# Third layer of a four-layer attention kernel: the self attention's values projected between its first steps, and queries that wait only for their own normed tokens

## The reference, cut to what matters

```python
def attention(x, ctx, ng, nbv, ncg, ncb, wq, wkv, wo, bo, rel_emb):
    xn = layer_norm(x, ng, nbv)
    cn = layer_norm(ctx, ncg, ncb)
    q = xn @ wq
    kv = cn @ wkv
    k, v = jnp.split(kv, 2, axis=-1)
    ...
    sim = jnp.einsum('bhnd,bhmd->bhnm', q, k)
    sim = (sim + rel_pos_bias(rel_emb, n, m)) * SCALE
    attn = jax.nn.softmax(sim, axis=-1)
    out = jnp.einsum('bhnm,bhmd->bhnd', attn, v)
    ...
    return out @ wo + bo
x = attention(x, x, sa_norm_g, ...) + x
x = attention(x, context, ca_norm_g, ...) + x
```

## Time and profile before

| what | value |
|---|---|
| median of 3 runs | 4007.54 us (3999.14, 4007.54, 4008.92) |
| the profiled execution's own time | 4000.44 us |
| its span, first to last instruction | 3998.7 us |
| TensorE busy | 3681.9 us, 92% of the span |
| VectorE, ScalarE, GpSimd busy | 1997.7 us, 1717.6 us, 381.1 us |
| mean clock granted to TensorE | 0.953 of full speed |
| turns of the third layer | between 2111 and 3230 us of the span, some 149 us each |

### The profile page before, as it was taken

How to read it: one execution, slowest core, us unless ns; L and a number is a source line. 1 busy time by engine, 2 the same in 40 slices (tenths; PEclk the granted TensorE clock), 3 DMA queues, 4 the chain that set the end, 5 groups by cost and what they waited for, 6 DMA issues and landing times. The chain is left out here.

```text
span 3998.7 us, 67495 instructions
## 1 busy us (share of the span) xinstructions
PE 3681.9 (92%) x21816; PEld 2836.5 (71%) x21816; DVE 1997.7 (50%) x6075; ACT 1717.6 (43%) x4729; POOL 381.1 (10%) x471
## 2 busy tenths in 40 slices
PE   7999999999979999999978999999999996888888
PEld 5878787877758888888756666666666664666666
DVE  3644555455525555555543454454454544555454
ACT  3544454444523433333314545545545552333333
POOL 1101110110011111111000000000000001111110
PEclk9999999999979999999989999999999997989898
DMA  5000000000030000000011000000000000000000
GB/s 177 4 11 14 14 4 11 14 12 6 1 114 11 12 12 12 12 12 10 3 42 44 8 7 14 8 7 14 8 7 14 7 1 26 13 12 12 20 15 5
DMA packets 69151, 75.08 MB, mean 19 GB/s; under 512 B 17537, under 2 KB 66561, under 8 KB 67841
## 3 DMA queue, kind: packets, MB, share of 16 engines
q1 hardware_dynamic: 68864, 71.42, 5.9%
HBM read 64.01 MB, written 7.40 MB: 18 GB/s over the span
## 5 line engine op out<-in xcount | busy, mean ns | idle before, releaser
L161 PE MATMUL l_bank<-l_xT,weights_of_layers_and 128*128 128x224 f32 x2816 | 625.5, 376 | 40.5 <-DMA weights_of_layers_and<-in_L_xattn_w_fused 11.8
L161 PEld LDWEIGHTS l_bank<-l_xT,weights_of_layers_and 128*128 128x128 f32 x2816 | 552.6, 202 | 70.5 <-DMA weights_of_layers_and<-in_L_xattn_w_fused 12.1
L614 ACT ACTIVATE l_pT<-l_bank 125x336 f32<-125x336 f32 (+2 forms) x608 | 290.8, 478 | 287.0 <-PE l_bank L546 276.7
L546 PEld LDWEIGHTS l_bank<-identity,l_p 112*125 112x125 f32 (+2 forms) x1952 | 272.8, 174 | 155.6 <-issue 77.8
L546 PE MATMUL l_bank<-identity,l_p 112*125 112x112 f32 (+2 forms) x1952 | 321.7, 277 | 24.6 <-DVE l_p L593 20.0
L161 PE MATMUL l_bank<-l_cT,weights_of_layers_and 128*128 128x375 f32 x832 | 319.9, 515 | 4.7 <-DVE l_z L1815 3.7
L335 PE MATMUL l_bank<-l_cv,l_pT 125*112 125x17 f32 (+1 forms) x2304 | 268.3, 247 | 45.5 <-ACT l_pT L377 44.1
L335 PEld LDWEIGHTS l_bank<-l_cv,l_pT 125*112 125x112 f32 x2304 | 261.1, 180 | 52.6 <-DVE l_O L419 26.6
L313 PEld LDWEIGHTS l_bank<-identity,l_p 112*125 112x125 f32 (+1 forms) x1408 | 218.7, 184 | 111.3 <-ACT l_p L373 11.2
L161 PE MATMUL l_bank<-weights_of_layers_and,l_cT 128*125 128x256 f32 (+2 forms) x960 | 295.7, 448 | 0.1
L728 POOL TENSOR_TENSOR l_ve<-l_mv,eps 112x2 f32<-112x2 f32 (+1 forms) x89 | 17.5, 196 | 2607.6 <-DVE l_mv L722 2607.6
(11 more groups left out here) (255 smaller groups left out, 6264.3 us busy)
## 6 DMA issues: line engine op xcount, KB each, us to landing
l_cx<-in_ctx SPq DMA_DIRECT2D x32, 375.0 KB
l_cT<-in_ctx_turned SPq DMA_DIRECT2D x32, 375.0 KB, 3.5
x_after_layer<-l_z SPq DMA_DIRECT2D x24, 224.0 KB, 2.4
l_x<-x_after_layer SPq DMA_DIRECT2D x24, 224.0 KB, 2.7
weights_of_layers_and<-in_L_xattn_w_fused SPq DMA_DIRECT2D x1, 2048.0 KB, 8.8
weights_of_layers_and<-in_L_xattn_w_ff SPq DMA_DIRECT2D x1, 2048.0 KB, 12.1
weights_of_layers_and<-in_L_xattn_lin_W SPq DMA_DIRECT2D x2, 1024.0 KB, 10.2
weights_of_layers_and<-in_L_xattn_sa_wkv SPq DMA_DIRECT2D x1, 2048.0 KB, 14.7
```

The lines of the kernel that those rows point to most:

```text
L161: last = pe.matmul(out, left, right, start=(k == 0), stop=(k == len(pairs) - 1))
L546: last = pe.transpose(TR.bank(m)[:ph.keys, g * ph.rows:(g + 1) * ph.rows], p[:ph.rows, m % self.p_slots, g * ph.keys:(g + 1) * ph.keys], i ...
L614: return act.activation(out, src, ACT.Copy)
```

## The change

The four value projections are no longer made behind the keys at the end of a turn (and ahead of the loop, for turn 0). They become jobs beside steps 0 to 3 of the self attention: `v00` in step 0, `v01` in step 1, `v10` in step 2 ahead of `ck00`, `v11` in step 3 ahead of `ck01`. TensorE projects them there, and ScalarE copies each behind the exponentials of its step. The ring's order of jobs changes with it, so each job's bank and the job that it waits for follow from the new order. The wait of the self attention's product with the values is now for this turn's copy.

The second edit gives the copy of `xT` a semaphore, `x_ready`, raised when its two instructions are done; the queries wait for it and no longer for `xcT` too.

```diff
-            return [P.got_before(f"v{j}{r // 2}")] if r % 2 == 0 else []
+            return [P.got(f"v{j}{r // 2}")] if r % 2 == 0 else []
...
+        for s in range(4):
+            beside_own[s] = [(f"v{s // 2}{s % 2}", "act")] + beside_own.get(s, [])
...
-        ending = [("k0", "act"), ("z1", "dve")] + [(f"k{t}", "act") for t in (1, 2, 3)] + [(f"v{j}{half}", "act") for j in range(PAIR) for half in range(2)]
+        ending = [("k0", "act"), ("z1", "dve")] + [(f"k{t}", "act") for t in (1, 2, 3)]
...
+        x_ready = signal("x_ready", 1)
...
             def queries(i, t):
-                project(pe, P, i, f"q{t}", [columns(V["sq"], 2 * t + n) for n in range(2)], xT, P.got("xT"))
+                project(pe, P, i, f"q{t}", [columns(V["sq"], 2 * t + n) for n in range(2)], xT, x_ready.this(0))
...
             def own_side(i, s):
+                if s < 4:
+                    values(i, s // 2, s % 2)
                 if 2 <= s <= 7:
                     context_keys(i, 0, s - 2)
...
                 if coming:
                     for t in (1, 2, 3):
                         keys(i, t)
-                    values(i)
...
-                for out, g, b in outs:
+                for n, (out, g, b) in enumerate(outs):
                     for t in range(KT):
                         last = act.activation(out[:, t, :], P.bank(name)[:, t * TP:(t + 1) * TP], ACT.Identity,
                                               scale=c.column[g][:, t:t + 1], bias=c.column[b][:, t:t + 1])
+                    if n + 1 < len(outs):
+                        last.then_inc(x_ready.sem, 1)
...
             def own_side(i, s):
-                if s == 10:
+                if s < 4:
+                    values(i, s // 2, s % 2)
+                elif s == 10:
                     context_values(i, 0, 0, 0)
```

More of the change, by code:

```diff
@@ L2201, in queries, with values @@
             def queries(i, t):
-                project(pe, P, i, f"q{t}", [columns(V["sq"], 2 * t + n) for n in range(2)], xT, P.got("xT"))
+                project(pe, P, i, f"q{t}", [columns(V["sq"], 2 * t + n) for n in range(2)], xT, x_ready.this(0))
             def keys(i, t):
                 project(pe, P, i, f"k{t}", [columns(V["skv"], 2 * t + n) for n in range(2)], xcT, P.got("xT"))
[L2207 to L2213, removed]
+            def values(i, j, half):
+                name, a = f"v{j}{half}", 1024 + 512 * half
+                for sem, count in P.free(i, name):
+                    pe.wait_ge(sem, count)
+                product(pe, P.bank(name)[:T, 0:512], [(xcT[:, kt, j * T:(j + 1) * T], V["skv"][:, kt, a:a + 512]) for kt in range(KT)]).then_inc(P.full.sem, 1)
             def own_side(i, s):
+                if s < 4:
+                    values(i, s // 2, s % 2)
                 if 2 <= s <= 7:
@@ L2290, in _ @@
                 keys(-1, t)
-            values(-1)
             with pe.Fori(0, TURNS - 1) as i:
@@ L2338, in keys, with values @@
                 move(i, f"k{t}", kT[:, 2 * t:2 * t + 2, :], 2 * TP)
[L2340 to L2343, removed]
+            def values(i, j, half):
+                move(i, f"v{j}{half}", v[:, j, 8 * half:8 * half + 8, 0:DH], 512, T)
             def own_side(i, s):
-                if s == 10:
+                if s < 4:
+                    values(i, s // 2, s % 2)
+                elif s == 10:
                     context_values(i, 0, 0, 0)
```

## The result

| | kernel before | changed kernel |
|---|---|---|
| median | 4005.4 us (16 runs) | 3967.91 us (16 runs) |
| ratio to before, 95% interval | | 0.9899 (0.9874 to 0.9925) |
| profiled execution: time, span | 4000.44, 3998.7 us | 3969.45, 3967.7 us |
| TensorE busy, share of the span | 3681.9 us, 92% | 3670.8 us, 93% |
| third layer, mean of turns 1 to 6 | 149.87 us | 144.69 us |

The forecast was 3968 us. The kernel is faster by 1.0%. The last row is the measure that I use for the experiments: from the first product of `k1` to `k3` in turn 1 to the same product in turn 7, divided by 6. In it the other layers have no part. Their time differs from one execution to the next by some microseconds: the turning of `xhat` that opens turn 0's work starts at 2116.48 us in the profile after and at 2111.69 in that of before, 4.8 us apart, though the change touches nothing ahead of it.

What follows compares the result with a forecast made beforehand. TensorE sets the pace, busy 1082.55 of 1119 us in the third layer's turns. Values 29.1 us plus queries 6.5 make 35.6, taken from the known times' mean 4004.0: 3968 us, range 3959 to 3987.

Steps and rivals of the forecast that it cites:

- The removed wait: TensorE's wait before turning probabilities (L546 for L593), put down to ScalarE's code loading: 20.0 us, to fall under 2 us.
- The stretch of 13.48 us if TensorE never waits: Values 6.86, three scores 2.70, `ck00` 1.44, through `ck01` 2.48; against measured windows the eight turns gain 29.1 us.
- The code of TensorE: Rival: TensorE waits for its own code at the loop's branch back; 12.9 us lost, 3981 us, chance 0.06.
- a first piece: TensorE's first code load after the branch: longest hidden before 4.34 us, now costing 0.42 us a turn, 2.5 in all.
- What is not moved: No DMA changes its queue place, no transfer is among TensorE's waits, and order after the second turning stays.
- the measure by the last wait: Time from TensorE's last wait ahead of its branch to the scores, available to hide code loading: 4.34 us before, 3.92 now.
- ScalarE's distances: From last copy's start, turns 1 to 6: first exponential 2.68 us later, second 2.15 after that, item 1's 5.96 after the copy.
- t0: The end of the keys' products on TensorE, 2424.59 in turn 2, from which the forecast counts turns 1 to 6.
- The cover: At `ck00`, the copy of `v00` frees the bank 1.09 us before TensorE needs it; one further ScalarE gap costs 6.4 us, chance 0.12.
- The mechanism that I named as the likeliest to fail: ScalarE's code loading comes out longer than the one-microsecond covers between its copies of values and TensorE's `ck00` and `ck01`.
- The queries: Queries start 0.85 us earlier by not waiting for `xcT`: 5.95 us in seven turns, 0.6 ahead of the loop, together 6.5.
- Given back in steps 4 to 8: Rival: VectorE or ScalarE sets the pace there, so TensorE comes earlier and waits; 3997 us, chance 0.05.

Runs made afterwards that it cites:

- the unrolled ScalarE: Kernel before with the third layer's loop written out on ScalarE alone; 3979.67 us, ratio 0.9947, 146.30 us a turn.
- the queries alone: Kernel before with only the new semaphore `x_ready` for the queries, values not moved; 3994.42 us, ratio 0.9979, turns alternating between 149.1 and 147.8 us.
- transfers later: Changed kernel with the sending of `x` and the next context's load held back until `ck00` of the next turn is copied; 3964.65 us, ratio 0.9902.

## Why the prediction was right

The forecast rested on 35.6 us; 35.9 were found. Point by point:

- **The removed wait.** Right: 20.0 us to none, stretch at a granted clock of 1.00 in all eight turns. That it was ScalarE's code after the branch is shown by the unrolled ScalarE and by its packets of code, which are gone with the branch. Its price by rows, 18.06 - 13.48 = 4.58 us a turn, is wait (3.0) and low clock (about 1.6 in this stretch), as the alternating turns show apart.
- **The stretch of 13.48 us if TensorE never waits.** Right in kind, 0.49 us a turn too long; measured 12.99 on average. The term was mis-sized at the scores and at `ck00`. Three score products take 2.70 us back to back and 0.78 to 0.87 each between value products; with all values in step 0, where two stand back to back, those take 1.57, so it is the third that is held up (it uses the bank of the first; that this is the reason is inferred). And `ck00` takes 1.26 us until the next instruction, where I had subtracted the wait from 2.30 and got 1.44: a row's end overlaps the next row's start. That is 3.9 us more gained than predicted in eight turns.
- **The code of TensorE.** I had "at most 0.42 us a turn" from a first piece and 2.15 from a second. Measured were gaps of 0.56, 0.60, 0.89, 0.53, 0.48, 0.66, in sum 3.7 us, and by the turns with the loops of both engines written out 0.75 each, 4.5 us, that the sum had at nothing. One of my own signs of being wrong, a gap on TensorE by "issue" at the loop's start, is there. The step that failed is under "What is not moved": no DMA changes its place in a queue, but the first scores behind the branch moved toward the transfers, from 10.6 us behind their first issue to 4.5 us, and with them held back the turn loses 144.38 - 143.94 = 0.44 us, about the 0.42 of the prediction. That agreement is no proof of the measure by the last wait, since the packet follows that wait by different times. A second packet of code came 0.4 to 1.0 us behind the first scores in each of these turns, but no gap followed it. The Trainium skill (Runtime: NRT & Kernel Launch, section Instruction fetch mechanics) has the rule that a taken branch forces a fetch if the target isn't in the loaded window; on both engines the traces agree, and unrolling takes the gaps away. A rival by a third, then, that came in at 4.5 of its 12.9 us.
- **Luck.** 3.9 us more gained at the scores and `ck00`, and up to 4.5 us lost at the branch, cancel. The total is better than its terms, and that the median came within 0.1 us of the forecast is chance: the 95% interval of the ratio is 20 us wide.
- **ScalarE's distances.** The first exponential came 4.24 us after the last copy, not 2.68, since the transfers fell on it (2.85 with them held back); the second gap was 0.89, not 1.67. The copy of `v00` ended at t0 + 7.36 (predicted 6.76), but TensorE's own gap moved `ck00` from t0 + 7.85 to 8.20. The cover, 1.09 forecast, was 0.84; at `ck01` it was 1.07 (copy of `v10` over at 2432.59), 1.1 forecast. The mechanism that I named as the likeliest to fail was used up in one turn as soon as TensorE's gap was removed.
- **The queries.** 6.5 forecast, 6.0 + 0.77 measured. The semaphore cost nothing.
- **Given back in steps 4 to 8.** Did not come: L563's waits are 4.8 us in place of 5.3.
- **Against the median.** I had set the time by the mean of the times known, 4004; over 16 runs the median of before is 4005.4, and with the 35.9 us taken off it would be 3969.5.

A better version exists by the turns: with TensorE's and ScalarE's loops of the third layer written out, 0.75 us a turn or 4.5 us are gained over the changed kernel. The interval of its ratio (0.9893 to 0.9926) can't tell it from the changed kernel (0.9874 to 0.9925).

## What to carry to other kernels

An idle gap that "issue" ends in every pass of a loop but the first points to code loading at the branch: try the loop unrolled on that one engine before moving work, and if it can't be, put long products behind the branch for an engine that waits for another, and keep transfers out of that time. Four long products ahead of the branch did not cover TensorE's own load, sixteen did. Price the branch for each engine apart, look in the view of the queues for the packet that brings the code, and read the loss from whole turns and not from the gaps alone. A wait of TensorE of some 3 us can cost half as much again in clock, in one turn and not in the next, so compare kernels by several turns.

## What the runs showed of the hardware

- TensorE's clock after equal waits: with the queries alone, waits of 2.9 to 3.2 us at the same place left it at 2.4 GHz in turns 2, 4 and 6 (windows at 1.00) and at 1.2 GHz for a part of turns 1, 3 and 5 (0.91 to 0.93), about 1.6 us of difference.
- The load of code at a taken branch: on TensorE 2.6 to 3.0 us from its packet of 16 KB to the first product where a gap shows it; on ScalarE three packets of 8 KB, and from the start of the last copy to the first exponential 2.7 to 3.0 us with the data queues quiet (kernel before, and transfers later), 4.0 to 4.4 with `x` and the context in flight.
